# A graph network in one kernel: GpSimd's indirect transfers, at most two under way

## The chip, the cores and the metric

One core of a Trainium2 chip. The metric is the device time of one execution in microseconds. The engines are TensorE (PE, with its weight loads as PEld), VectorE (DVE), ScalarE (ACT), GpSimd (POOL) and SyncE (SP); 16 DMA engines move data between HBM and the on-chip memory (SBUF).

## What is computed

Four layers over 3750 nodes of 256 features and 60000 edges, each added to its input:

```python
x = x + _L0_gnn_ref(_layernorm(x), W, attn_l, attn_r, h_bias, src, dst, edge_type_8)  # attention over edges
x = x + _L0_ffn_ref(_layernorm(x)[None], ...)[0]                                     # shared MLP + 2 of 4 experts
x = x + _L1_gnn_ref(_layernorm(x), edge_attr_20, ..., edge_index)                    # convolution over edges
x = x + _L1_ffn_ref(_layernorm(x)[None], ...)[0]                                     # 2 of 16 experts
```

The two graph layers:

```python
feat_all = jnp.einsum('ni,rhid->rnhd', inputs, conv_weights)       # 8 relations, 4 heads of 64
e = leaky_relu(sum(feat_all[typ, src] * attn_l[typ]) + sum(feat_all[typ, dst] * attn_r[typ]))
alpha = softmax of e over the edges of each dst, per head
h = segment_sum(alpha * feat_all[typ, src], dst) + h_bias

filt = silu(rbf @ Wf1 + bf1) @ Wf2 + bf2                           # per edge
msg = x[col] * filt;  agg = segment_sum(msg, row)                  # then an MLP and a batch norm
```

## The kernel before

**Tiles.** Nodes lie in 30 tiles of 128. Edges are sorted on the chip into bins by the tile of their target node (for the attention) and of their source node (for the convolution). A bin is padded to a multiple of 512 edges, so that a group of `K = 4` tiles of 128 edges belongs to one node tile. A table of sorted edge records has `ET = 588` tiles, 147 groups. `fill` and `fill1` first write both tables with empty records (L541 to L548): all of them carry one and the same row address, 3750 in the first table and 0 in the second. Places that no edge takes stay so, some at the end of each bin and a longer stretch at the end of the table.

**Who moves rows.** All gathers and scatters by computed address are indirect transfers that GpSimd issues, one for 128 rows:
- `Sender` (L276) scatters edge records into a table, a column of 128 edges at a time, in batches of 8 on two semaphores in turn, so that up to 16 are under way. For table 0 it sends 20 columns beside `rank` "by_src", 44 in the first layer norm (beside `fill1`, 28 writes of 252 KB, L1956) and 405 in `project`. For table 1 it sends the last 37 columns in `mixture`.
- `project` (L603) computes the features of all nodes and relations into `feat` in HBM, with 30 stores of 1040 KB from SyncE (L639). It ends when its engines and its sender have ended.
- `attend` (L726) runs through the 147 groups as a software pipeline over steps. GpSimd gathers four tiles of `feat` rows (128 x 260 floats, 130 KB) into one of three buffers `got` (L806), and scatters three columns of table 1 (L812) per group from the fourth group on. The gathers of a group wait until the group three before it has been used up: `f_ready` from DVE (L925, which reads the buffer's first half) and `last_ready` from ACT (L957, the second half). One semaphore for each buffer counts its four gathers. DVE reads the gathered rows first at L895.
- `convolve` (L1331) gathers four tiles of `xtab` rows (128 x 256 floats, 128 KB) per group (L1402), again into three buffers, after both of DVE's multiplications L1507 of the group three before (`msg_ready`). TensorE's largest part is L1454.
- `routed` (L1646) scatters token numbers to `slots` (L1710, 60 transfers, batches of 10), gathers 76 tiles of tokens (L1788, two buffers) and combines the results with 60 gathers (L1891, 12 buffers).

**Order.** Every engine has a program of its own, with waits on semaphores written out by hand. A stage ends in a barrier of all engines. GpSimd runs its transfers in the order written. Its instruction ends when the descriptors have been made, and the data land later; the transfer then adds 16 to its semaphore.

## Time and profile before

| | |
|---|---|
| median of 3 runs | 4172.16 us (4170.39 to 4174.0) |
| profiled execution | 4176.44 us, span 4174.7 us |
| busy | PE 2928.3, PEld 2364.7, DVE 2177.3, ACT 1210.5, POOL 2277.2 us |
| granted TensorE clock, mean | 0.858 of full |
| DMA | 317.71 MB, 76 GB/s |

The stages in the span, roughly: edge keys and ranks to 103 us, first layer norm to 165, projection to 700, attention to 2030, join and first feed-forward layer to 2420, convolution to 3300, update and routing to 3620, experts to 4079, combination and store to the end. The busy time of GpSimd is that of making descriptors. A share of busy time over the whole span says little here, as each stage has a limit of its own. In the rows below, "idle before" an instruction is put down to what released it; "issue" means that the profile shows nothing that it waited for.

### The profile page before, as it was taken

The numbers are of one execution on the slowest core, as the hardware profiler recorded it, in microseconds if no ns is written. First come the engines' busy times: TensorE is split into PE (matmuls) and PEld (weight loads), VectorE is DVE, ScalarE is ACT, GpSimd is POOL, SyncE is SP. The second block draws the span as 40 slices with busy tenths as digits, with TensorE's granted clock in tenths as the row PEclk, the third lists the DMA queues.
The fourth block names the chain that finished last, engine by engine and source line by source line (L and its number), as shares of the span: only waits on it lengthen the run. The fifth ranks groups of instructions, "written<-read, shape, count | busy, mean of one in ns | idle before, by whom it ended". The sixth has DMA issues, their size and how long they took to land. (4 is left out here: it accounts for less than half of the span.)

```text
span 4174.7 us, 73619 instructions
## 1 busy us (share of the span) xinstructions
PE 2928.3 (70%) x20296; PEld 2364.7 (57%) x20297; DVE 2177.3 (52%) x5961; ACT 1210.5 (29%) x3266; POOL 2277.2 (55%) x2336
## 2 busy tenths in 40 slices
PE   5199101777777777776379679999999864299990
PEld 1188101555555555555255358888888633288990
DVE  8411002877777777777743557777777444011112
ACT  1123000444444444444223223333333231022220
POOL 2777775777777777777240056666666200511115
PEclk8599655998998999999679789999999875599995
DMA  3344101222222222225100143333335501155533
GB/s 105 108 135 137 40 2 32 63 65 63 63 64 63 64 64 63 64 64 62 23 19 1 47 136 89 90 89 90 90 90 84 52 0 39 49 175 173 171 104 114
DMA packets 209214, 317.71 MB, mean 76 GB/s; under 512 B 63367, under 2 KB 150063, under 8 KB 208388
## 3 DMA queue, kind: packets, MB, share of 16 engines
q0 software_dynamic: 95008, 179.89, 19.9%
q1 hardware_dynamic: 103204, 127.24, 9.4%
q10 hardware_dynamic: 10944, 9.97, 0.7%
q8 instruction: 17, 0.28, 0.0%
q14 instruction: 41, 0.34, 0.0%
HBM read 248.03 MB, written 68.84 MB: 76 GB/s over the span
## 5 line engine op out<-in xcount | busy, mean ns | idle before, releaser
L1402 POOL DMA_INDIRECT conv_got<-xtab,conv_rowidx x588 | 565.8, 962 | 313.2 <-DVE conv_msg L1507 156.6
L806 POOL DMA_INDIRECT att_got<-feat,att_rowidx x588 | 573.2, 975 | 201.5 <-issue 150.2
L294 POOL DMA_INDIRECT table<-l0a_rec,l0a_addr x469 | 458.2, 977 | 216.7 <-issue 146.1
L1454 PE MATMUL conv_pf<-conv_wf,conv_act 128*128 128x256 f32 x2352 | 534.0, 380 | 0.2 <-DVE conv_filt L1502 0.2
L812 POOL DMA_INDIRECT table<-recs_rec,recs_addr x432 | 423.2, 980 | 131.6 <-issue 130.4
L1454 PEld LDWEIGHTS conv_pf<-conv_wf,conv_act 128*128 128x128 f32 x2352 | 447.6, 190 | 76.9 <-issue 0.8
L982 PE MATMUL att_pmax<-all_identb,att_away 128*128 128x512 bf16 x588 | 261.1, 444 | 203.9 <-DVE att_elo L901 203.2
L863 DVE TENSOR_REDUCE att_tmax<-att_pmax 128x4 f32<-128x512 f32 x588 | 373.8, 680 | 31.1 <-PE att_pmax L986 27.6
L986 PE MATMUL att_pmax<-all_identb,att_ehi 128*128 128x128 bf16 x2352 | 383.6, 242 | 0.0
L986 PE MATMUL att_pmax<-all_identb,att_elo 128*128 128x128 bf16 x2352 | 383.3, 242 | 0.0
L1420 ACT ACTIVATE conv_act<-conv_p,conv_bf 128x512 f32<-128x512 f32 x294 | 186.2, 684 | 552.1 <-PE conv_p L1446 552.1
L1502 DVE TENSOR_TENSOR conv_filt<-conv_pf,conv_bf 128x512 f32<-128x512 f32 x294 | 202.8, 691 | 222.1 <-PE conv_pf L1454 222.1
L986 PEld LDWEIGHTS att_pmax<-all_identb,att_elo 128*128 128x128 bf16 x2352 | 260.5, 111 | 93.0 <-issue 41.6
L1013 PE MATMUL att_psum<-att_f,att_onehot 128*128 128x260 f32 x1176 | 303.7, 403 | 1.9 <-DVE att_f L925 1.9
L1873 DVE TENSOR_TENSOR moe_hid<-moe_gatev,moe_p 128x512 f32<-128x512 f32 x76 | 52.2, 687 | 484.4 <-ACT moe_gatev L1853 484.4
L1825 PE MATMUL moe_p<-moe_xT,moe_w 128*128 128x128 f32 x2432 | 287.5, 277 | 17.4 <-issue 7.1
L957 ACT ACTIVATE att_f<-att_got,att_ex 128x64 f32<-128x64 f32 x1176 | 294.5, 333 | 0.0
L1825 PEld LDWEIGHTS moe_p<-moe_xT,moe_w 128*128 128x128 f32 x2432 | 278.7, 193 | 23.5 <-issue 18.3
L1463 PE MATMUL conv_psum<-conv_msg,conv_onehot 128*128 128x256 f32 x1176 | 279.0, 380 | 5.6 <-DVE conv_msg L1507 5.6
L1788 POOL DMA_INDIRECT moe_got<-xtab,moe_tokens x76 | 72.0, 948 | 368.2 <-PE moe_pT L1814 358.6
L706 PE MATMUL proj_ps<-proj_w,proj_xs 128*128 128x260 f32 x960 | 220.1, 388 | 74.6 <-DVE proj_wr L652 70.0
L986 PEld LDWEIGHTS att_pmax<-all_identb,att_ehi 128*128 128x128 bf16 x2352 | 260.0, 111 | 0.0
(336 smaller groups left out, 5074.0 us busy)
## 6 DMA issues: line engine op xcount, KB each, us to landing
moe_w<-in_L_ffn_w SPq DMA_DIRECT2D x96, 512.0 KB
feat<-proj_out SPq DMA_DIRECT2D x30, 1040.0 KB
results<-moe_y ACTq DMA_DIRECT2D x76, 128.0 KB, 1.7
att_got<-feat,att_rowidx POOLq DMA_INDIRECT x588
conv_got<-xtab,conv_rowidx POOLq DMA_INDIRECT x588, 2.8
xtab<-ln_row SPq DMA_DIRECT2D x60, 128.0 KB, 1.7
table<-l0a_rec,l0a_addr POOLq DMA_INDIRECT x469
table<-recs_rec,recs_addr POOLq DMA_INDIRECT x469, 2.1
```

The costliest lines, as they stand in the source:

```text
L294: self.nc.gpsimd.indirect_dma_start(out=self.table, out_offset=bass.IndirectOffsetOnAxis(ap=self.addrs[:, j:j + 1], axis=0), in_=self.recs ...
L806: nc.gpsimd.indirect_dma_start(out=got[g % 3][:, k, :], out_offset=None, in_=feat, in_offset=bass.IndirectOffsetOnAxis(ap=rowidx[:, g * K ...
L812: nc.gpsimd.indirect_dma_start(out=table1, out_offset=bass.IndirectOffsetOnAxis(ap=addr1[:, i:i + 1], axis=0), in_=rec1[:, i, :], in_offse ...
L863: count(v.tensor_reduce(tmax[:, k, :], pmax[k][:, :, :], AX.X, ALU.max))
L957: nc.scalar.activation(f[s2][:, k, h, 0:HD], got[s2][:, k, h * HD:(h + 1) * HD], ACT.Copy, scale=ex[:, k, h:h + 1]).then_inc(last_ready, 1)
L982: nc.tensor.matmul(pmax[k][:, :, :], away[s1][:, k, :], bcast(c["identb"][:, :], [[0, HEADS], [1, P]]), start=True, stop=False, skip_group ...
L986: ins = nc.tensor.matmul(pmax[k][:, h, :], part[s1][:, k, h:h + 1].broadcast_to([P, P]), c["identb"][:, :], start=False, stop=(part is elo ...
L1013: ins = nc.tensor.matmul(psum[:, 0:HEADS * H1], oh[s2][:, k, :], flat(f[s2][:, k, :, :]), start=(k == 0), stop=(k == K - 1))
L1402: nc.gpsimd.indirect_dma_start(out=got[g % 3][:, k, :], out_offset=None, in_=xtab, in_offset=bass.IndirectOffsetOnAxis(ap=rowidx[:, g * K ...
L1454: ins = nc.tensor.matmul(pf[b][:, k, :], act1[s3][:, h, (2 * b + k) * P:(2 * b + k + 1) * P], wf2[:, h, :], start=(h == 0), stop=(h == 1))
L1463: ins = nc.tensor.matmul(psum[s4][:, 0:D], oh[s4][:, k, :], msg[s4][:, k, :], start=(k == 0), stop=(k == K - 1))
L1825: ins = nc.tensor.matmul(ps[w][:, j * P:(j + 1) * P], wt[w][:, k, j * P:(j + 1) * P], xT[w][:, k, :], start=(k == 0), stop=(k == 1))
```

## The change

A class `Transfers` keeps the list of the indirect transfers that GpSimd has begun in a stage, each with its semaphore and the count at which it has landed. `room()`, called before a transfer, waits for the landing of the one two before it; `begun()` enters it. It is used in `Sender`, `attend`, `convolve` and the `send` stage of `routed`, and not in the `moe` and `comb` stages. So that each of two transfers under way can be waited for by itself, every tile of a gathered group gets its own semaphore (`got_s[slot][k]`), and the scatters alternate between semaphores. DVE waits for the four semaphores of a group one by one; ACT's wait for the gathered rows is gone. The waits for free buffers are split: in `attend` the first two gathers wait for `f_ready` and the last two for `last_ready`; in `convolve` each pair waits for one of the two `msg_ready` of the group three before. In each of these places the wait for the buffer stands first and `room()` after it.

```diff
+class Transfers:
+    LIMIT = 2
+    def __init__(self, pool):
+        self.pool, self.counts, self.order = pool, {}, []
+    def room(self):
+        if len(self.order) >= self.LIMIT:
+            self.pool.wait_ge(*self.order[-self.LIMIT])
+    def begun(self, name, sem):
+        self.counts[name] = self.counts.get(name, 0) + 16
+        self.order.append((sem, self.counts[name]))
 class Sender:
-    BATCH = 8
...
+        under_way = Transfers(pool)
+        for i in range(self.columns):
+            j, u = self.first + i, i % Transfers.LIMIT
+            under_way.room()
+            self.nc.gpsimd.indirect_dma_start(
+                out=self.table, out_offset=..., in_=self.recs[:, j, :], in_offset=None).then_inc(self.sent[u], 16)
+            under_way.begun(u, self.sent[u])
...
 attend, gpsimd:
+            under_way = Transfers(pool)
             for g in range(GROUPS):
-                if g >= SLOTS:
-                    pool.wait_ge(f_ready, g - 2)
-                    pool.wait_ge(last_ready, (g - 2) * LAST)
                 for k in range(K):
+                    if g >= SLOTS and k == 0:
+                        pool.wait_ge(f_ready, g - 2)
+                    if g >= SLOTS and k == ON_DVE:
+                        pool.wait_ge(last_ready, (g - 2) * LAST)
+                    under_way.room()
                     nc.gpsimd.indirect_dma_start(
-                        out=got[g % 3][:, k, :], ...).then_inc(got_s[g % 3], 16)
-                if g >= 2 * SLOTS:
-                    pool.wait_ge(sent[g % 3], 16 * ROUND * (g // 3 - 1))
+                        out=got[g % 3][:, k, :], ...).then_inc(got_s[g % 3][k], 16)
+                    under_way.begun((g % 3, k), got_s[g % 3][k])
                 for i in range(max(g - SLOTS, 0) * ROUND, max(g - SLOTS + 1, 0) * ROUND):
+                    under_way.room()
                     nc.gpsimd.indirect_dma_start(
-                        out=table1, ...).then_inc(sent[g % 3], 16)
+                        out=table1, ...).then_inc(sent[i % 3], 16)
+                    under_way.begun(i % 3, sent[i % 3])
 attend, vector:
-                    dve.wait_ge(got_s[s1], ((i + 1) if u else i) * 16 * K)
+                    for k in range(K):
+                        dve.wait_ge(got_s[s1][k], ((i + 1) if u else i) * 16)
 attend, scalar:
-                    act.wait_ge(got_s[s2], ((i + 1) if u == 2 else i) * 16 * K)
 convolve, gpsimd:
+            under_way = Transfers(pool)
             for g in range(GROUPS):
-                if g >= SLOTS:
-                    pool.wait_ge(msg_ready, (g - 2) * 2)
                 for k in range(K):
+                    if g >= SLOTS and k % 2 == 0:
+                        pool.wait_ge(msg_ready, (g - SLOTS) * 2 + k // 2 + 1)
+                    under_way.room()
...
 convolve, vector:
-                    dve.wait_ge(got_s[s3], i * 16 * K)
+                    for k in range(K):
+                        dve.wait_ge(got_s[s3][k], i * 16)
 routed, send, gpsimd:
+                under_way = Transfers(pool)
                 for i in range(2 * NT):
-                    if batch >= 2 and i % BATCH == 0:
-                        pool.wait_ge(sent[batch % 2], 16 * BATCH * (batch // 2))
+                    under_way.room()
```

## Rows read from the trace of the kernel before

**Rows 1.** Page, part 5: GpSimd's costliest groups (busy, mean ns, idle before).
```profile
L1402 POOL DMA_INDIRECT conv_got<-xtab,conv_rowidx x588 | 565.8, 962 | 313.2 <-DVE conv_msg L1507 156.6
L806 POOL DMA_INDIRECT att_got<-feat,att_rowidx x588 | 573.2, 975 | 201.5 <-issue 150.2
L294 POOL DMA_INDIRECT table<-l0a_rec,l0a_addr x469 | 458.2, 977 | 216.7 <-issue 146.1
L812 POOL DMA_INDIRECT table<-recs_rec,recs_addr x432 | 423.2, 980 | 131.6 <-issue 130.4
```
**Rows 2.** Windows by stage: length, then each engine's busy time; clock; DMA share; GB/s.
```profile
206.00:442.00 236.00, 227.93 (x1074) 196.76 (x1073) 44.18 (x120) 69.39 (x177) 178.10 (x186) 1.00 0.43 136
442.00:688.00 246.00, 0.00 (x0) 0.00 (x0) 0.00 (x0) 0.00 (x0) 184.28 (x192) 0.50 0.03 3
725.00:1873.00 1148.00, 826.52 (x8782) 659.08 (x8780) 883.03 (x3096) 487.17 (x1673) 874.05 (x897) 0.92 0.27 64
2442.00:3180.00 738.00, 738.00 (x3792) 633.18 (x3791) 532.45 (x1139) 258.18 (x506) 487.70 (x508) 1.00 0.35 90
3180.00:3285.00 105.00, 104.66 (x536) 89.40 (x534) 72.24 (x153) 35.45 (x68) 66.60 (x69) 1.00 0.81 79
```
**Rows 3.** Waits: total us, times, longest.
```profile
DVE att_z L895 <- DMA att_got<-feat,att_rowidx: 221.8, 127, 4.1
...
POOL att_got L806 <- ACT att_f L957: 34.5, 94, 6.1
```
**Rows 4.** Timeline of GpSimd and DVE in the attention: start, us, instruction.
```profile
1509.81 0.95 POOL L806 DMA_INDIRECT att_got<-feat,att_rowidx  x1 [0.30 <-issue]
1512.71 0.17 DVE L895 TENSOR_TENSOR att_z<-att_ers,att_got 128x16 f32<-128x16 f32 x1 [1.54 <-DMA att_got<-feat,att_rowidx]
1514.91 0.98 POOL L806 DMA_INDIRECT att_got<-feat,att_rowidx  x1 [0.30 <-issue]
...
1523.82 0.98 POOL L806 DMA_INDIRECT att_got<-feat,att_rowidx  x1 [0.30 <-issue]
```
**Rows 5.** Landing: page part 6; tiles conv_got (2442:3180, 2600:2604, 3225:3284) and comb_got.
```profile
table<-recs_rec,recs_addr POOLq DMA_INDIRECT x469, 2.1
...
DMA to landing us min/median/max: 2.6/2.8/5.3
DMA to landing us min/median/max: 3.9/4.1/4.6
DMA to landing us min/median/max: 10.0/13.4/14.4
DMA to landing us min/median/max: 2.7/2.7/2.8
```
**Rows 6.** Timeline in the convolution: DVE's messages and GpSimd behind them.
```profile
2701.62 1.28 DVE L1507 TENSOR_TENSOR conv_msg<-conv_filt,conv_got 128x512 f32<-128x512 f32 x2
2703.18 0.95 POOL L1402 DMA_INDIRECT conv_got<-xtab,conv_rowidx  x1 [1.08 <-DVE conv_msg L1507]
...
2709.01 0.95 POOL L1402 DMA_INDIRECT conv_got<-xtab,conv_rowidx  x1 [1.08 <-DVE conv_msg L1507]
```
**Rows 7.** Timeline at the attention's fourth group: ACT, then GpSimd.
```profile
723.13 2.00 ACT L957 ACTIVATE att_f<-att_got,att_ex 128x64 f32<-128x64 f32 x8
725.91 0.94 POOL L806 DMA_INDIRECT att_got<-feat,att_rowidx  x1 [6.11 <-ACT att_f L957]
```
**Rows 8.** Windows around one store of `feat`, and GpSimd's scatters beside it.
```profile
229.00:230.00 1.00, 1.00 (x6) 0.85 (x6) 0.00 (x0) 0.39 (x1) 0.70 (x2) 1.00 0.64 198
...
232.00:233.00 1.00, 1.00 (x6) 0.86 (x5) 0.00 (x0) 0.51 (x2) 0.96 (x1) 1.00 0.73 187
228.24 0.96 POOL L294 DMA_INDIRECT table<-l0a_rec,l0a_addr  x1 [0.31 <-issue]
...
230.77 0.96 POOL L294 DMA_INDIRECT table<-l0a_rec,l0a_addr  x1 [0.30 <-issue]
```
**Rows 9.** Windows of the first layer norm.
```profile
103.00:125.00 22.00, 4.12 (x20) 3.86 (x20) 18.67 (x50) 4.31 (x11) 16.49 (x18) 0.51 0.96 329
145.00:158.00 13.00, 0.00 (x0) 0.00 (x0) 0.00 (x0) 0.00 (x0) 9.76 (x11) 0.50 0.03 2
```

More of the change, by code:

```diff
@@ L283, in __init__ @@
         self.first, self.columns = first, columns
-        self.sent = [s.sem(f"sent{u}") for u in range(2)]
+        self.sent = [s.sem(f"sent{u}") for u in range(Transfers.LIMIT)]
     def __call__(self, pool):
-        batches = [range(i, min(i + self.BATCH, self.columns)) for i in range(0, self.columns, self.BATCH)]
-        done = [0, 0]
-        for n, batch in enumerate(batches):
-            u = n % 2
-            wait_positive(pool, self.sent[u], done[u])
-            for i in batch:
-                j = self.first + i
-                self.nc.gpsimd.indirect_dma_start(
-                    out=self.table, out_offset=bass.IndirectOffsetOnAxis(ap=self.addrs[:, j:j + 1], axis=0),
-                    in_=self.recs[:, j, :], in_offset=None).then_inc(self.sent[u], 16)
-            done[u] += 16 * len(batch)
-        for u in range(2):
-            wait_positive(pool, self.sent[u], done[u])
+        under_way = Transfers(pool)
[3 more added lines that the diff above has]
+            self.nc.gpsimd.indirect_dma_start(
+                out=self.table, out_offset=bass.IndirectOffsetOnAxis(ap=self.addrs[:, j:j + 1], axis=0),
+                in_=self.recs[:, j, :], in_offset=None).then_inc(self.sent[u], 16)
+            under_way.begun(u, self.sent[u])
+        for u in range(Transfers.LIMIT):
+            wait_positive(pool, self.sent[u], 16 * len(range(u, self.columns, Transfers.LIMIT)))
 def layer_norm(nc, name, c, x_res, xnT, table=None, add=False, side=None, fill=None):
@@ L766, in attend @@
         loaded, prep, dv = s.sem("loaded"), s.sem("prep"), s.sem("dv")
-        got_s = [s.sem(f"got_s{u}") for u in three]
+        got_s = [[s.sem(f"got_s{u}{k}") for k in range(K)] for u in three]
         oh_ready, turned, ohT_ready, away_ready = (s.sem(n) for n in ("oh_ready", "turned", "ohT_ready", "away_ready"))
@@ L1364, in convolve @@
         filt_ready, msg_ready, summed, agg_done = (s.sem(n) for n in ("filt_ready", "msg_ready", "summed", "agg_done"))
-        got_s = [s.sem(f"got_s{u}") for u in three]
+        got_s = [[s.sem(f"got_s{u}{k}") for k in range(K)] for u in three]
         block = s.block()
@@ L1396, in _ @@
             pool.wait_ge(prep, 2)
+            under_way = Transfers(pool)
             for g in range(GROUPS):
[L1399 to L1400 removed]
                 for k in range(K):
+                    if g >= SLOTS and k % 2 == 0:
+                        pool.wait_ge(msg_ready, (g - SLOTS) * 2 + k // 2 + 1)
+                    under_way.room()
                     nc.gpsimd.indirect_dma_start(
                         out=got[g % 3][:, k, :], out_offset=None, in_=xtab,
[L1404 removed]
+                        in_offset=bass.IndirectOffsetOnAxis(ap=rowidx[:, g * K + k:g * K + k + 1], axis=0)).then_inc(got_s[g % 3][k], 16)
+                    under_way.begun((g % 3, k), got_s[g % 3][k])
         @block.scalar
@@ L1693, in routed @@
         with Stage(nc, "send") as s:
-            BATCH = 10
-            assert 2 * NT % (2 * BATCH) == 0
-            sent, dv = [s.sem(f"sent{u}") for u in range(2)], s.sem("dv")
+            LANES = Transfers.LIMIT
+            assert 2 * NT % LANES == 0
+            sent, dv = [s.sem(f"sent{u}") for u in range(LANES)], s.sem("dv")
             block = s.block()
@@ L1704, in _ @@
             def _(pool):
+                under_way = Transfers(pool)
                 for i in range(2 * NT):
-                    t, k, batch = i // 2, i % 2, i // BATCH
+                    t, k = i // 2, i % 2
                     n = P if t < NT - 1 else TAIL
-                    if batch >= 2 and i % BATCH == 0:
-                        pool.wait_ge(sent[batch % 2], 16 * BATCH * (batch // 2))
+                    under_way.room()
                     nc.gpsimd.indirect_dma_start(
                         out=slots, out_offset=bass.IndirectOffsetOnAxis(ap=addr_i[0:n, k * NT + t:k * NT + t + 1], axis=0),
-                        in_=token[0:n, t:t + 1], in_offset=None).then_inc(sent[batch % 2], 16)
-                for u in range(2):
-                    pool.wait_ge(sent[u], 16 * NT)
+                        in_=token[0:n, t:t + 1], in_offset=None).then_inc(sent[i % LANES], 16)
+                    under_way.begun(i % LANES, sent[i % LANES])
+                for u in range(LANES):
+                    pool.wait_ge(sent[u], 16 * (2 * NT // LANES))
         with Stage(nc, "moe") as s:
```

7 lines of the change are left out of this document (3 added, 4 removed).

## Prediction

> **What bounds the kernel now.** I read the page first, for the GpSimd groups: four lines issue 2,077 of the indirect transfers, each busy for 0.96 to 0.98 us [rows 1]. I then cut the span by stage, to see who is full in each [rows 2]. In the projection (206 to 442) TensorE is full, but the stage goes on to 688 with GpSimd alone. In the attention (725 to 2016) no compute engine is full: DVE 77%, TensorE 72%. In the convolution (2442 to 3285) TensorE is busy all the time. The waits settle the attention: GpSimd's gaps are mostly "issue" (it waits for nothing) [rows 1], while DVE waits 221.8 us for gathers [rows 3]. The timeline shows the beat [rows 4]: a transfer each 1.25 to 1.30 us, say 1.27, seven in a group of 8.91 us (1514.91 to 1523.82). So GpSimd's issue bounds the attention and the tail of the projection. In the convolution GpSimd waits 156.6 us for DVE's messages [rows 1]: four transfers of 1.25 and a gap of 0.78 make 5.84 us (2703.18 to 2709.01 [rows 6]), which is TensorE's time.
>
> **The limit, in general.** A transfer may begin when the one two before it has landed. Without the limit two transfers take 2 x 1.27 = 2.54 us, so it costs nothing as long as landing plus waking GpSimd stay under that. Landing is counted from the instruction's start. A gather takes 2.8 us in the convolution and 2.7 in the last stage, a scatter 2.1 [rows 5]. For the attention's gather the trace gives no landing, but DVE's L895 starts at 1512.71 on the one issued last, at 1509.81 [rows 4]: 2.90 with DVE's own start, so 2.8 again.
>
> Waking has two prices. A transfer with one wait starts 0.28 us after its releaser's end: DVE ends at 2702.90, GpSimd starts at 2703.18 [rows 6]. With two waits, where the one written second comes last (L804, `last_ready`, at the fourth group), ACT ends at 725.13 and GpSimd starts at 725.91: 0.78 us [rows 7]. My reading is that the first wait rides on the transfer, already handed to the engine, and the second stops the hand-over, so that it begins only when the wait is met. That counts here: in the diff the buffer wait is written first and `room()` second, at k = 0 and 2 in both stages.
>
> So the distance from a transfer to the next but one is at least:
> - scatter, one wait: 2.1 + 0.28 = 2.4 us, under 2.54: free.
> - gather, one wait: 2.8 + 0.27 = 3.07 us.
> - gather, limit as second wait: 2.8 + 0.77 = 3.57 us.
> - scatter, limit as second wait: 2.1 + 0.78 = 2.9 us.
>
> **Attention.** One group in order, G for gather, S for scatter: G0 at 0; G1 at 1.27; G2, whose second wait is G0's landing, at 3.57; G3 1.27 later, 4.84; S0 waits for G2, 3.57 + 3.07 = 6.64; S1 7.91; S2 9.18; the next G0 has S1's landing as its second wait, 7.91 + 2.9 = 10.8. That is 10.8 in place of 8.91, +1.88 us in each of 144 groups: +271 us. All of it is on the path, since nothing but GpSimd bounds the stage. The first three groups issue no scatters and their 12 gathers take some 3 us longer, but GpSimd idled 6.11 us behind them [rows 7], which covers it. The half-group waits take away only waits that cost little now (34.5 us in all [rows 3], nearly all as normal 0.30 gaps): nothing gained.
>
> Some gathers land late. The last 100 us of the convolution land at 13.4 us, and four gathers at 2599 to 2603 at 4.1 [rows 5]. These are groups of padding, whose rows all carry the same address (the memsets of the empty tables), at the end of the table and at the end of a bin. I take about 28 such groups in each stage: 16 at the end (3183 to 3283) and the rest at the ends of bins (an estimate: landings like the two shown recur at the ends of bins). Alone such a gather takes some 3.75 us, so each of the two pairs in a group costs 0.95 more: 28 x 1.9 = +53 us. Attention: +324 us; bounds +197 (below) and +347.
>
> **Convolution.** A group is two pairs, each opened by a gather with `room()` as second wait: 2 x 3.57 = 7.14 us, against 5.84 of TensorE. GpSimd becomes the bound: +1.28 x 144 = +184 us. Padding groups: 28 x 1.8 = +50, but the 16 at the end already run at some 6.6 us now, 0.76 over the beat, so -12. And the last gather landed up to 14.4 us after its issue where it will take 4: -10. Sum +212 us.
>
> **Projection and first layer norm (`Sender`).** Each transfer has one wait and a landing of 2.1 us: free, except beside large transfers. Line 639 stores 1040 KB 30 times; in one store the DMA engines are 0.64 busy and more for four microseconds, 229 to 233 [rows 8]. The scatter issued at 228.24 and the one after it land only when it is over, at about 233.4 (estimate: the end of that stretch and a little). Now GpSimd goes on issuing at 230.77; with the limit it starts at 233.4 + 0.28, 2.9 us later. Over the phases at which a store can begin I take 2.5, bounds 2.3 and 3.3: 30 x 2.5 = +75 us (69 to 99), all on the path, as GpSimd ends this stage alone [rows 2]. In the layer norm 18 scatters run beside the fill of table 1, DMA share 0.96 [rows 9]; a landing of 3.4 us (estimate, between 2.1 and 5.2) makes each 0.5 longer: +8 us, and there too GpSimd is the last one working, 145 to 158.
>
> **Edits at nothing.** `Sender` beside `rank` and in the mixture: 20 and 37 transfers behind DVE and TensorE work. The 60 scatters to `slots`: single wait, 2.1 us landing, DMA engines idle. Their first and last waits are the old ones. DVE's four semaphores in place of one: three more waits a group, at some 0.05 to 0.1 us each, on an engine that waits for the gathers anyway; if that cover went, 147 x 0.2 = 30 us a stage. ACT's wait taken away: `ex_ready` implied it. The combine stage has no limit and stays as it is.
>
> **Sum.** 324 + 212 + 75 + 8 = 619 us on the profiled execution's 4176.4 gives 4795.6; the median of the runs is 4.3 us below that execution, so 4791.
>
> **A rule of the skill.** The trace's gather of 128 KB takes 2.8 us, in two stages [rows 5]. The Trainium skill, DMA: Bandwidth & Descriptors, section Anatomy of one DMA, gives about 2.0 us plus the bytes by 436 GB/s for a transfer from GpSimd, 2.3 us for this one. The trace does not agree; by the page's figure the pairs would be 2.57 and 3.07 us, and the whole about 4500 (the attention +128 and 53 for padding, the convolution +43 and 28, the senders 83). The same page (section Latency and other measured facts) says that a lighter load on HBM makes the fixed part smaller. Both make the third rival.
>
> **Rivals.**
> 1. The limit's wait costs 0.28 everywhere (as if it were the one that rides on the transfer). For it: only one place in the trace shows the 0.78. Against: the delay is clean there. The attention's group is then 9.93 us (+1.0 x 144 = 147, with padding 197), the convolution's 6.12 (+40, with padding and end 68): 4172 + 197 + 68 + 83 = 4520 us. Chance 0.13.
> 2. TensorE's clock. In the attention it is 0.92 of full with TensorE 72% busy; in the convolution 1.00 at 100% [rows 2]. With GpSimd as bound, TensorE is at 59% and 82%. If the clock went as in the attention's present rows, work in the half-speed stretches doubles, still below the new groups. Should a fifth of the groups run at 1.2 GHz throughout, TensorE would need 12.8 us a group in the attention (826.52 of 1148 us is 6.4 of 8.91, doubled) and 11.7 in the convolution: 29 x (2.0 + 4.6) = +191, about 4980 us. Chance 0.06.
> 3. Landing depends on how many transfers are under way. With two, a gather might land in 2.3 us; then the pairs are 2.57 (one wait) and 3.07 (two), the attention's group 9.8 and the convolution's 6.14, and the time about 4500. Chance 0.04. Not slower at all: from a landing of 2.54 - 0.77 = 1.77 us on, the limit never decides for a gather, nor under 2.26 where it is the one wait; the time stays 4172. Against both: the landings are 2.6 at the least over the whole regular stretch, gaps in GpSimd's issue included, and the gathers of the last stage, up to twelve at once, land in 2.7 [rows 5]; depth does not show. Chance of the second 0.02.
> 4. The change does not limit (waits met in advance). The counts in `Transfers` ask for the full 16 per transfer, so no. Chance 0.01, 4172.
>
> **How the numbers follow.** Forecast as summed, 0.74. Its own range: low, 0.6 us in place of 0.77 for the second wait and landings of 2.7 (some -130); high, the upper bounds of padding and stores (+23, +24) and 30 for DVE: 4660 to 4870. For 8 in 10 I reach a little towards rivals 1 and 2: 4620 to 4890. A measurement of this kernel tells 0.2% apart. Faster than that 0.01, within it 0.03, slower 0.96.
>
> **What would show it.** Right: attention groups 10.8 us apart and convolution groups 7.1; GpSimd's gaps in them put down to its own transfers' landing, not "issue"; gaps at k = 2 longer than at k = 1; scatters in 442 to 688 still 1.27 apart; TensorE no longer full in the convolution. Wrong: groups at 9.9 and 6.1 (rival 1), TensorE full with a clock near 0.5 (2), gathers landing much under 2.7 (3).

## Result: slower by 15.9%, and the profile after

| | before | after |
|---|---|---|
| median | 4171.27 us (4 runs, 4166.4 to 4174.0) | 4833.34 us (4 runs, 4829.8 to 4837.9) |
| ratio | | 1.159, interval 1.157 to 1.161 |
| profiled execution, span | 4176.44, 4174.7 us | 4831.86, 4830.1 us |
| granted clock of TensorE, mean | 0.858 | 0.828 |

The instructions and the bytes are the same (317.74 MB against 317.71), and the busy times of DVE, ACT and GpSimd moved by less than 30 us. TensorE's grew from 2928.3 to 3136.8 us, under a granted clock of 0.828 in place of 0.858; it is not what bounds the long stages now, as the windows below show. What made the kernel longer are GpSimd's gaps. First the page of the changed kernel, part 5, GpSimd's groups (busy, mean ns, idle before, releaser), and part 6, the time from issue to landing. The lines answer to [rows 1] and [rows 5].

```profile
PE 3136.8 (65%) x20296; PEld 2445.8 (51%) x20297; DVE 2174.6 (45%) x5961; ACT 1217.9 (25%) x3266; POOL 2305.3 (48%) x2336
...
L1421 POOL DMA_INDIRECT conv_got<-xtab,conv_rowidx x588 | 572.2, 973 | 527.9 <-DMA conv_got<-xtab,conv_rowidx 430.8
L822 POOL DMA_INDIRECT att_got<-feat,att_rowidx x588 | 564.7, 960 | 407.1 <-DMA att_got<-feat,att_rowidx 219.3
...
L307 POOL DMA_INDIRECT table<-l0a_rec,l0a_addr x469 | 456.4, 973 | 314.9 <-issue 130.3
L828 POOL DMA_INDIRECT table<-recs_rec,recs_addr x432 | 455.7, 1055 | 258.1 <-DMA att_got<-feat,att_rowidx 193.5
...
att_got<-feat,att_rowidx POOLq DMA_INDIRECT x588, 2.8
conv_got<-xtab,conv_rowidx POOLq DMA_INDIRECT x588, 2.8
...
table<-recs_rec,recs_addr POOLq DMA_INDIRECT x469, 2.1
```

GpSimd's idle time ahead of these four groups is 1508.0 us (527.9 + 407.1 + 314.9 + 258.1), where it was 863.0 [rows 1]: 645.0 more, and the profiled execution is 655.4 us longer. The releaser has changed from "issue" to GpSimd's own gathers. The landings are what they were.

The timeline of GpSimd over one group of the attention, in the changed kernel. It is the beat that [rows 4] showed for before.

```profile
1502.83 0.97 POOL L822 DMA_INDIRECT att_got<-feat,att_rowidx  x1 [0.48 <-issue]
1504.11 0.96 POOL L822 DMA_INDIRECT att_got<-feat,att_rowidx  x1 [0.30 <-issue]
1506.39 0.95 POOL L822 DMA_INDIRECT att_got<-feat,att_rowidx  x1 [1.33 <-DMA att_got<-feat,att_rowidx]
1507.65 0.95 POOL L822 DMA_INDIRECT att_got<-feat,att_rowidx  x1 [0.30 <-issue]
1509.42 1.00 POOL L828 DMA_INDIRECT table<-recs_rec,recs_addr  x1 [0.82 <-DMA att_got<-feat,att_rowidx]
1510.72 0.97 POOL L828 DMA_INDIRECT table<-recs_rec,recs_addr  x1 [0.30 <-DMA att_got<-feat,att_rowidx]
1512.00 1.20 POOL L828 DMA_INDIRECT table<-recs_rec,recs_addr  x1 [0.30 <-issue]
1513.65 0.97 POOL L822 DMA_INDIRECT att_got<-feat,att_rowidx  x1 [0.46 <-issue]
```

Read the starts as distances from the first: 0, 1.28, 3.56, 4.82, 6.59, 7.89, 9.17, and the next group at 10.82. The forecast was 0, 1.27, 3.57, 4.84, 6.64, 7.91, 9.18, 10.8. The 1.33 us of idle time at the third gather is the limit behind a second wait; the 0.82 at the first scatter is the limit as the only wait.

What the other engines make of it, in windows of the changed kernel by stage (length, then busy time of PE, PEld, DVE, ACT and POOL, clock, DMA share, GB/s; they answer to [rows 2]):

```profile
206.00:442.00 236.00, 227.43 (x1060) 196.04 (x1061) 46.63 (x118) 68.99 (x176) 118.96 (x124) 0.98 0.41 131
442.00:790.00 348.00, 4.12 (x22) 3.51 (x20) 1.47 (x4) 0.77 (x2) 253.84 (x265) 0.51 0.04 6
830.00:2240.00 1410.00, 905.36 (x8596) 714.88 (x8596) 872.53 (x3036) 484.33 (x1642) 879.61 (x880) 0.84 0.21 51
...
2880.00:3730.00 850.00, 760.75 (x3584) 586.09 (x3583) 489.71 (x1070) 245.28 (x480) 457.37 (x471) 0.98 0.27 73
```

In the projection's first window GpSimd issues 124 transfers where it issued 186 [rows 2]; the missing 62 are sent when nobody else works any more. The stage boundaries, read from GpSimd's first and last instruction of each line, put the loss in its places:

| stretch | before, us | after, us | difference | forecast |
|---|---|---|---|---|
| first layer norm to the projection's sender | 103.3 to 165.2 | 103.7 to 173.1 | +7.5 | +8 |
| projection, to the first gather of the attention | to 704.2 | to 800.7 | +88.6 | +75 |
| attention and what follows, to the convolution | to 2422.0 | to 2863.9 | +345.4 | +324 |
| convolution and update, to `slots` | to 3537.4 | to 4192.1 | +212.8 | +212 |
| rest | to the end | to the end | +0.7 | 0 |

### The profile page after: what moved, and what is told of

Its sections match the earlier page's. It is cut to its first block and busy times, and to the rows that moved or that the text cites. A ratio compares the mean times of both kernels' runs of the same rounds, so it can differ in the third digit from the quotient of the medians.

```text
span 4830.1 us, 74107 instructions
## 1 busy us (share of the span) xinstructions
PE 3136.8 (65%) x20296; PEld 2445.8 (51%) x20297; DVE 2174.6 (45%) x5961; ACT 1217.9 (25%) x3266; POOL 2305.3 (48%) x2336
## 2 busy tenths in 40 slices
DMA packets 209217, 317.74 MB, mean 66 GB/s; under 512 B 63367, under 2 KB 150063, under 8 KB 208388
## 5 line engine op out<-in xcount | busy, mean ns | idle before, releaser
L1421 POOL DMA_INDIRECT conv_got<-xtab,conv_rowidx x588 | 572.2, 973 | 527.9 <-DMA conv_got<-xtab,conv_rowidx 430.8
L822 POOL DMA_INDIRECT att_got<-feat,att_rowidx x588 | 564.7, 960 | 407.1 <-DMA att_got<-feat,att_rowidx 219.3
L999 PE MATMUL att_pmax<-all_identb,att_away 128*128 128x512 bf16 x588 | 315.6, 537 | 466.8 <-DVE att_elo L919 466.7
L307 POOL DMA_INDIRECT table<-l0a_rec,l0a_addr x469 | 456.4, 973 | 314.9 <-issue 130.3
L828 POOL DMA_INDIRECT table<-recs_rec,recs_addr x432 | 455.7, 1055 | 258.1 <-DMA att_got<-feat,att_rowidx 193.5
L1003 PE MATMUL att_pmax<-all_identb,att_ehi 128*128 128x128 bf16 x2352 | 463.5, 274 | 0.0
L1003 PE MATMUL att_pmax<-all_identb,att_elo 128*128 128x128 bf16 x2352 | 461.5, 274 | 0.0
L1528 DVE TENSOR_TENSOR conv_msg<-conv_filt,conv_got 128x512 f32<-128x512 f32 x294 | 191.7, 693 | 449.9 <-DMA conv_got<-xtab,conv_rowidx 449.9
L1003 PEld LDWEIGHTS att_pmax<-all_identb,att_elo 128*128 128x128 bf16 x2352 | 303.4, 129 | 127.8 <-issue 102.8
L1483 PEld LDWEIGHTS conv_psum<-conv_msg,conv_onehot 128*128 128x128 f32 x1176 | 225.8, 201 | 183.5 <-issue 154.9
L999 PEld LDWEIGHTS att_pmax<-all_identb,att_away 128*128 128x128 bf16 x588 | 73.3, 125 | 479.7 <-DVE att_elo L919 479.7
L1003 PEld LDWEIGHTS att_pmax<-all_identb,att_ehi 128*128 128x128 bf16 x2352 | 302.2, 128 | 0.0
L1847 PE MATMUL moe_p<-moe_xT,moe_w 128*128 128x128 f32 x2432 | 288.6, 277 | 16.8 <-issue 10.8
L1010 PE MATMUL att_pT<-all_identb,att_away 128*128 128x128 bf16 x588 | 63.0, 235 | 359.7 <-ACT att_away L968 359.7
```

The source lines that it names most:

```text
L307: self.nc.gpsimd.indirect_dma_start(out=self.table, out_offset=bass.IndirectOffsetOnAxis(ap=self.addrs[:, j:j + 1], axis=0), in_=self.recs ...
L822: nc.gpsimd.indirect_dma_start(out=got[g % 3][:, k, :], out_offset=None, in_=feat, in_offset=bass.IndirectOffsetOnAxis(ap=rowidx[:, g * K ...
L828: nc.gpsimd.indirect_dma_start(out=table1, out_offset=bass.IndirectOffsetOnAxis(ap=addr1[:, i:i + 1], axis=0), in_=rec1[:, i, :], in_offse ...
L999: nc.tensor.matmul(pmax[k][:, :, :], away[s1][:, k, :], bcast(c["identb"][:, :], [[0, HEADS], [1, P]]), start=True, stop=False, skip_group ...
L1003: ins = nc.tensor.matmul(pmax[k][:, h, :], part[s1][:, k, h:h + 1].broadcast_to([P, P]), c["identb"][:, :], start=False, stop=(part is elo ...
L1421: nc.gpsimd.indirect_dma_start(out=got[g % 3][:, k, :], out_offset=None, in_=xtab, in_offset=bass.IndirectOffsetOnAxis(ap=rowidx[:, g * K ...
```

## Experiments

Kernels of one batch ran on one chip, beside the kernel before; every ratio is to the kernel before of the same batch. This matters: swap, limit3, sender_only and no_limit ran on a chip on which the kernel before takes 4172 us. The other kernels ran on two chips on which the same kernel before takes 5252 to 5277 us. Times of different batches on the first kind of chip are compared directly, as the kernel before takes 4171 to 4172 us in both; otherwise only where the text says so. Line numbers differ by a few between the kernels.

### Is the second wait the dearer one? (swap)

```diff
+                    under_way.room()
                     if g >= SLOTS and k == 0:
                         pool.wait_ge(f_ready, g - 2)
                     if g >= SLOTS and k == ON_DVE:
                         pool.wait_ge(last_ready, (g - 2) * LAST)
-                    under_way.room()
```
The same in `convolve`. The waits are the same ones, in the other order.

> The changed kernel with room() written ahead of the wait for the buffer, in the attention (k = 0 and 2) and in the convolution (k = 0 and 2). The limit of two stays. Theory (the wait written second stops the hand-over and costs 0.78 us in place of 0.28): the attention's group falls from 10.8 to about 9.95 us, the convolution's from 7.05 to about 6.15, and the time from 4833 to about 4560 us. Rival (the place of a wait does not matter, all is landing time): groups and time stay, 4833 us.

Measured: 4620.22 us, ratio 1.1075 (1.1057 to 1.1094), so 213 us less than the changed kernel for two lines exchanged. The convolution's groups are 6.07 us apart (7.05 in the changed kernel); the attention's 10.36 (10.89), where 9.95 was expected. The timeline of swap tells what the attention kept, first GpSimd, then DVE:

```profile
1502.51 1.08 POOL L822 DMA_INDIRECT att_got<-feat,att_rowidx  x1 [0.30 <-issue]
1503.89 0.96 POOL L822 DMA_INDIRECT att_got<-feat,att_rowidx  x1 [0.31 <-ACT att_f L974]
1505.63 0.94 POOL L822 DMA_INDIRECT att_got<-feat,att_rowidx  x1 [0.78 <-DMA att_got<-feat,att_rowidx]
...
1511.30 1.20 POOL L828 DMA_INDIRECT table<-recs_rec,recs_addr  x1 [0.30 <-issue]
1512.81 1.09 POOL L822 DMA_INDIRECT att_got<-feat,att_rowidx  x1 [0.30 <-issue]
```
```profile
1510.98 0.69 DVE L929 TENSOR_TENSOR att_onehot<-all_ramp,att_recs 128x512 f32<-128x512 f32 x1
1511.59 0.85 DVE L865 SCALAR_TENSOR_TENSOR l_acc<-l_acc,att_keep,att_psum 128x65 f32 x4
1512.36 0.68 DVE L943 TENSOR_TENSOR att_f<-att_got,att_ex 128x512 f32<-128x512 f32 x1
```

The idle time at the third gather is 0.78 us where it was 1.33. Part of that difference is the longer first gather beside it (1.08 us). From the landing of the gather two before to the start of the third, the two traces have 0.77 us with the limit as second wait and 0.26 with the limit written first, in the median of the attention's groups whose landing is recorded, and 0.76 and 0.26 in the convolution. So the price of the second wait is 0.51 us a place, where [rows 7] against [rows 6] gave 0.50. But the third scatter now takes 1.20 us and the first gather 1.08, where the others take 0.94 to 1.0. In the changed kernel the scatter was as long, yet a wait of the next gather covered it; here it is on the path. DVE works without a break beside it.

### Is it DVE that makes the scatter long? (swap_small_oh)

```diff
-  v.tensor_tensor(oh[u][:, :, :], bcast(c["ramp"][:, 0:P], [[0, K], [1, P]]), ...
+  kk = K if isinstance(t, int) else 1
+  v.tensor_tensor(oh[u][:, 0:kk, :], bcast(c["ramp"][:, 0:P], [[0, kk], [1, P]]), ...
```

> The kernel of the run swap; in the attention's loop DVE writes one tile of the one-hot matrix per group in place of four (128 elements in place of 512), so the other three keep the contents of an earlier group and the result is not the reference's. Theory (in swap the third scatter of each group takes 1.2 us in place of 0.96, because DVE's one-hot, accumulation and L943 then run without a gap; GpSimd's own descriptor work is what stands on the path there): the third scatter falls to under 1.1 us and the attention's group from 10.36 to 10.1 to 10.2 us; 4590 us. Rival (the length of the third scatter has nothing to do with DVE): 1.2 us and 10.36 us stay.

Measured: the third scatter takes 0.971 us in the mean, against 1.215 in swap. The groups are 12.1 us apart here, so DVE no longer works beside that scatter in every group, and the two means alone would not separate the length of DVE's run from its place. The trace does: 52 of the attention's transfers lie beside the four accumulations (L865 above; at least 0.8 us of them), and these take 0.976 us in the mean, where 140 such in swap take 1.224. With a quarter of the one-hot ahead of it, DVE's run no longer stretches a transfer. The kernel before has such transfers too, 44 of them, up to 1.48 us long, 1.107 in the mean.

The time, 4881.3 us in one run on a chip of the second kind, says nothing on the 30 us that I expected from it beside swap: there TensorE has idle time in the attention that the profile puts down to nothing (129.7 us at att_per, 51.0 at att_pT), as the last part of this section shows. It does say that swap's order of the waits did not bring this kernel under the changed kernel on such a chip (4874.93 us, below).

### How deep must the queue be? (limit3, limit1)

```diff
-    LIMIT = 2
+    LIMIT = 3
```

> The changed kernel with LIMIT = 3. Theory (only landing plus waking against the issue of the transfers between counts): three issues take 3.8 us, more than the 3.57 us of a gather with the dearer wait, so the regular groups are back at 8.9 and 5.84 us; left are the padding groups (some 30 us) and the scatters beside the stores of feat (some 50 us): about 4250 us. Rival (the waits themselves slow GpSimd down, whatever the depth): attention groups clearly above 9 us, time over 4400 us.

Measured: 4261.63 us, ratio 1.0219 (1.0202 to 1.0236). Attention groups are 8.90 us apart and convolution groups 5.84, both as before. What is left of the 90 us is 45.7 in the projection, whose stores still hold up the third transfer, and the padding: the last 16 groups take 10.5 us in the attention and 6.68 in the convolution. One transfer more gives back 86% of the loss (572 of 662 us).

```diff
-    LIMIT = 2
+    LIMIT = 1
```

> The changed kernel with LIMIT = 1: every transfer waits for the landing of the one before. Theory (distance = landing plus waking, 3.07 us for a gather, 3.57 where the limit is the second wait behind a gather, 2.4 for a scatter, 2.9 as second wait): attention group 2.9 + 3.07 + 3.57 + 3.07 + 3.07 + 2.4 + 2.4 = 20.5 us, convolution group 3.57 + 3.07 + 3.57 + 3.07 = 13.3 us, a scatter of the projection each 2.4 us; the time 4172 + 1670 + 1075 + 200 (padding) + 507 (senders) + 68 (slots) = about 7690 us. Rival (landing shortens when only one transfer is under way): landings clearly under 2.6 us, groups of 18 us or less.

Measured: 7819.87 us in one run. Attention groups 20.89 us apart (20.5 expected), convolution groups 13.04 (13.3). The convolution's gathers as a tile, in the changed kernel over the regular stretch and in limit1 over all:

```profile
L1421 POOL DMA_INDIRECT conv_got<-xtab,conv_rowidx x471: 940/946/1467, 2879.4 to 3729.8; - x157
...
DMA to landing us min/median/max: 2.7/2.8/4.4
```
```profile
L1421 POOL DMA_INDIRECT conv_got<-xtab,conv_rowidx x588: 944/944/1267, 4850.4 to 6868.4; - x196
...
DMA to landing us min/median/max: 2.6/2.8/4.0
```

A gather lands after 2.8 us whether it is alone, one of two, or one of three. More than three were never under way in the regular stretches of the kernel before either, at a landing of 2.8 us and a beat of 1.27, whatever its buffers allowed. The third rival falls.

### Projection and senders alone (sender_only)

```diff
 attend, convolve, gpsimd:
-                    under_way.room()
-                    under_way.begun((g % 3, k), got_s[g % 3][k])
+                if g >= 2 * SLOTS:
+                    pool.wait_ge(sent[g % 3], 16 * ROUND * (g // 3 - 1))
```
The limit stays in `Sender` and in `send`.

> The changed kernel without the limit in the attention and the convolution (their semaphores and half-group waits stay); the limit of two stays in Sender and in the scatters to slots. Theory: only the projection and the first layer norm are longer, by the 96 us by which the attention starts later in the changed kernel: about 4268 us. My forecast had 83 us here: 4255. Rival (the delay of the attention's start comes from something else in the change): 4172 us.

Measured: 4260.86 us, 1.0219 (1.0202 to 1.0236), 89 us over before, 7 under the expectation. The attention starts at 802.6 us, 98.4 later than before, so some ten come back later. That limit3 gives the same ratio is a coincidence of other parts: 45.7 us by the attention's start there, 98.4 here.

### The rest of the diff alone (no_limit)

```diff
-                    under_way.room()
-                    under_way.begun(...)
 Sender, send: as in the kernel before
```
What stays: a semaphore for each gather, the waits for half the buffers, DVE's four waits and ACT's missing one.

> The change without its limit anywhere: one semaphore for each gathered tile, DVE's four waits, ACT's wait gone, half-group waits; senders as before. Theory (these edits cost nothing): 4172 us, within 0.2%. Rival a (DVE's three more waits in each group count, some 0.2 us in the convolution and the attention): up to 4230 us. Rival b (the half-group waits help): under 4160 us.

Measured: 4164.1 us, 0.9993 (0.9972 to 1.0015). These edits cost nothing, as costed, and what they bring is within the interval: the median is 8 us under the kernel before, and in the trace the stretch from the end of the attention's last scatter to the convolution's first gather takes 396.3 us in place of 405.0. The whole loss is the limit's.

### Padding with one and the same address (spread_after, spread_before)

```diff
+  nc.gpsimd.iota(spread_i[:, :], pattern=[[0, 1]], base=0, channel_multiplier=29)
-  nc.gpsimd.memset(empty0[:, :, 0:1], float(NODES))
+  nc.gpsimd.tensor_copy(empty0[:, :, 0:1], bcast(spread[:, :], [[0, ET], [0, 1]]))
+  nc.gpsimd.tensor_copy(empty1[:, :, NG:NG + 1], bcast(spread[:, :], ...))
```
The empty records of a tile now point to 128 different rows; their edges still count for nothing.

> The changed kernel, but the empty records of both tables carry 128 different row addresses (29 times the partition) in place of one and the same. Theory (the late gathers are those of padding, whose 128 rows all lie at one address): all gathers land in 2.6 to 2.9 us, groups at the end of the tables are as long as the others (10.85 and 7.05 us), and the time falls by about 28 x 2.3 + 28 x 1.7 = 112 us, to about 4720. Rival (the end of the stages is slower for another reason, such as the queue or the number of rows): 4833 us and 13.1 us groups at the end.

Measured: 4771.32 us on the second kind of chip. The last 16 groups are 10.99 us apart in the attention and 7.12 in the convolution, as the regular ones; in the changed kernel they are 13.1 and 8.78. The tile of the convolution's gathers near the end of the table, the changed kernel first (gathers, their first and last start; how long the later ones waited for them; landing), then spread_after:

```profile
L1421 POOL DMA_INDIRECT conv_got<-xtab,conv_rowidx x48: 940/945/1215, 3779.8 to 3878.8; - x48
...
  POOL conv_got L1421: 50.9, 36
...
DMA to landing us min/median/max: 2.7/3.6/4.2
```
```profile
L1428 POOL DMA_INDIRECT conv_got<-xtab,conv_rowidx x60: 940/946/1462, 3779.8 to 3884.0; - x60
...
  POOL conv_got L1428: 35.7, 28
```

The changed kernel sends 48 gathers in 99 us, spread_after 60 in 104. So the one shared address is the cause. Against the unaltered changed kernel on another chip of this kind (4874.93 us, below) it is 104 us, where the two padding terms of my sum, 53 and 50, make 103.

> The kernel before with the same 128 addresses in the empty records. Theory: in the attention nothing changes, since GpSimd issues at its own beat whatever the landing; in the convolution the last gathers land in 2.8 us in place of 14, and TensorE stays the bound: 10 to 15 us less, 4160 us. If late landing cost the kernel before more than its last gather: under 4140 us.

Measured: 5329.07 us, against 5252.47 for the kernel before on that chip, ratio 1.015 (1.008 to 1.023). I had expected 4160 for a kernel before of 4172. That is 77 us more than the kernel before on its chip, and not the 10 to 15 less of the theory. Nothing in the edit explains a number of 5300; the kernel before itself took 1080 us more on this chip. That opened the question of the next part.

### The same kernels on another chip (round2, best, after_again, robust)

round2 is the kernel before with two scatters a group in the attention in place of three; best is no_limit with that and with the spread addresses; robust is swap with LIMIT = 3, two scatters a group and the spread addresses; after_again is the changed kernel, unaltered.

```diff
-ROUND = 3
+ROUND = 2
```

> The kernel before with ROUND = 2: two scatters of table 1 per group of the attention in place of three, 181 in place of 37 behind it in the mixture. Theory (the attention is bound by the number of transfers that GpSimd issues): the group is 6 x 1.27 = 7.63 us in place of 8.91, -182 us; the mixture's sender needs 230 us and ends some 38 us after the mixture ends now: about 4030 us. Rival (DVE or TensorE is close behind GpSimd in the attention): groups over 8.2 us, time over 4100 us.

> The kernel of the run no_limit with ROUND = 2 and with 128 different addresses in the empty records. Theory: the gain of round2 and 10 to 15 us from the convolution's end: about 4015 us.

> The changed kernel once more, unaltered, timed beside the kernel before, because in two jobs, with five other kernels, the kernel before took 5252 and 5260 us and no longer 4172, with stretches in which TensorE stands still without a wait. Theory (the chips differ: on some, many transfers under way hold up the other engines, most of all while the projection's scatters run): where before takes 4172 us the changed kernel takes 4833; where before takes about 5250 us it takes 4830 to 4900, and is the faster one. Rival (such a chip slows every kernel alike): there it would take 5250 x 1.159 = 6085 us.

> The changed kernel with LIMIT = 3, room() ahead of the buffer waits, 128 different addresses in the empty records, and ROUND = 2 (two scatters per attention group, 181 in the mixture). Theory: landing plus waking (3.07 us) is under three issues (3.8), so the attention's group is 6 x 1.27 = 7.63 us and the convolution's 5.84; the senders beside the stores cost 46 us. Where before takes 4172 us: 4172 + 46 - 182 + 38 - 12 = 4062 us. Where before takes 5250 us: below the changed kernel, some 4400, if three transfers under way are few enough to leave TensorE alone; if they are not, stalls of TensorE without a wait and over 4800.

| kernel | transfers allowed under way | us | ratio to before on its chip |
|---|---|---|---|
| before | up to 16 | 5252 to 5277 | 1 |
| spread_before | up to 16 | 5329.07 | 1.015 (1.008 to 1.023) |
| round2 | up to 16 | 5117.35 | 0.973 (0.967 to 0.979) |
| best | up to 16 | 5061.49 | 0.961 (0.955 to 0.967) |
| robust | 3 | 5008.64 | 0.948 (0.943 to 0.952) |
| after_again | 2 | 4874.93 | 0.924 (0.921 to 0.928) |
| spread_after | 2 | 4771.32 | 0.909 (0.904 to 0.914) |

The times that I had expected of round2 (4030 us) and best (4015) were for a chip of the first kind, and these runs don't test them. Their groups are not 7.63 us apart: 11.4 in round2, 11.2 in best, 11.6 in robust.

On such a chip the change makes the kernel faster by 7.6%, the same text that makes it slower by 15.9% on the first. The changed kernel itself moved by 0.9% between the two kinds (4833.34 to 4874.93), the kernel before by 26%. After_again's groups are 10.90 and 7.05 us apart, as on the first chip.

Where the kernels without a limit lose it is in the waits of TensorE put down to "issue", that is to nothing that the profile shows (total us, times, longest). First spread_before, then round2, then best:

```profile
PE proj_ps L713 <- issue: 392.9, 8, 75.7
PE att_pmax L993 <- issue: 265.8, 309, 1.9
```
```profile
PE proj_ps L706 <- issue: 407.0, 8, 75.7
...
PE att_pmax L986 <- issue: 213.2, 319, 1.3
```
```profile
PE proj_ps L713 <- issue: 406.3, 8, 75.6
...
PE att_pmax L994 <- issue: 81.0, 125, 1.2
```

And with the limit, robust (3) first, then after_again (2):

```profile
PE att_pmax L1010 <- issue: 52.2, 110, 1.1
...
PE proj_ps L726 <- issue: 3.9, 23, 0.4
```
```profile
PE att_pmax L999 <- issue: 89.1, 67, 4.7
...
PE proj_ps L719 <- issue: 2.8, 18, 0.2
```

In the projection's matmuls, 393 to 407 us of it become 3.9 and 2.8. With one under way (limit1, a chip of the second kind too) no row of the attention or the projection has it. The timeline of TensorE in the projection shows what it means, spread_before first, after_again below:

```profile
287.55 8.85 PE L713 MATMUL proj_ps<-proj_w,proj_xs 128*128 128x260 f32 x28 [48.59 <-issue]
...
388.37 7.94 PE L713 MATMUL proj_ps<-proj_w,proj_xs 128*128 128x260 f32 x28 [74.95 <-issue]
```
```profile
238.32 7.28 PE L719 MATMUL proj_ps<-proj_w,proj_xs 128*128 128x260 f32 x32 [0.16 <-issue]
```

The gaps of 49 to 75 us look like idle time without a cause, but ACT's and DVE's copies of the products tell what TensorE stood for. ACT copies the first five products of a node tile, DVE the last three; here they are in spread_before between two of TensorE's runs:

```profile
320.69 0.39 ACT L687 ACTIVATE proj_out<-proj_ps 128x260 f32<-128x260 f32 x1 [10.11 <-remote]
...
343.09 0.39 ACT L687 ACTIVATE proj_out<-proj_ps 128x260 f32<-128x260 f32 x1 [10.81 <-remote]
354.29 0.39 ACT L687 ACTIVATE proj_out<-proj_ps 128x260 f32<-128x260 f32 x1 [10.81 <-remote]
...
376.69 0.43 DVE L667 COPY proj_out<-proj_ps 128x260 f32<-128x260 f32 x1 [10.77 <-remote]
387.89 0.43 DVE L667 COPY proj_out<-proj_ps 128x260 f32<-128x260 f32 x1 [10.77 <-remote]
```

A product is four matmuls, so by TensorE's records seven of the eight products were done at 296.40 (287.55 + 8.85). Each copy waits for its product's count on one semaphore ("remote": the profile finds no instruction that ended just before the count rose). The counts come 11.20 us apart, the one for the seventh product 80 us after its matmuls; in after_again the copies start 0.88 us apart. Each copy starts 0.03 us after its count, and TensorE's next run starts at 388.37, 0.05 us after the copy of the last product, which gives it its buffer back. So TensorE does wait, for DVE, and DVE and ACT wait for TensorE's own signals, which reach them late or belong to products that were late; as the ends of matmuls are modelled, the trace doesn't tell these two apart. When the last scatter has been issued, at 727, the stage is back at its old beat within some 35 us.

And the windows of spread_before over the stage (columns as above):

```profile
182.00:727.00 545.00, 72.84 (x252) 58.94 (x252) 27.17 (x32) 15.29 (x40) 408.72 (x404) 0.55 0.09 21
727.00:952.00 225.00, 177.91 (x828) 153.29 (x828) 42.11 (x99) 54.83 (x140) 1.08 (x1) 0.90 0.34 119
```

As long as GpSimd sends its 404 transfers, TensorE is busy 72.84 us of 545. It does three quarters of its instructions after them, so that work which lay side by side now lies end to end, and the attention begins at 952.5 us where it began at 704.2. With two under way TensorE is at its full 232.13 us of 254:

```profile
206.00:460.00 254.00, 232.13 (x1080) 200.00 (x1080) 48.77 (x123) 69.46 (x178) 130.39 (x134) 0.96 0.39 127
```

What is shown: on these chips TensorE's signals come up to 80 us after the matmuls, and TensorE stands for up to 76 us for that, while GpSimd issues its scatters in one unbroken row; it does not in the projection of the kernels with a limit. Why the signals are late stays open. Against a late supply of instructions speaks that each copy, and TensorE's next run, starts within 0.05 us of what it waits for.

Nor do the runs show that it is the number under way. The steps by which a landing scatter counts up its semaphore come 1.94 us after its start in the median in spread_before and 2.00 in the kernel before, and the beat is 1.27 us in both, so away from the stores of `feat` two are under way, with the limit and without it; "up to 16" in the table is what the kernel allows. Nor is it enough that the limit puts a wait ahead of each transfer, even where it is met in advance. Robust's `Sender` has these waits in the mixture too. There its 181 scatters go out 1.28 us apart without a break, and TensorE has the same steps of 11.2 us again: it restarts at 2801.2, 2812.5, 2823.7, 2834.9 and 2846.1. One of these rows:

```profile
2823.67 1.54 PE L1233 MATMUL mixf_bank<-mixf_h,mixf_e2w 128*64 128x384 f32 x2 [9.66 <-issue]
```

What the disturbed stretches share is the unbroken beat; in the projection of the kernels with a limit the stores break it. That is a reading: no run breaks the beat and changes nothing else.

The table isn't a scale of depth either. Robust, whose projection is undisturbed, took 1727 us from the attention's first gather to its last where after_again took 1664, with groups of 11.6 us for an expected 7.63. From there to the convolution's first gather it took 621 us against 441: its mixture sends 181 scatters and not 37, and TensorE has idle time put down to nothing there (117.6 us in the mixture's matmuls, up to 43.7 at a time). My reading for robust (4400 if three were few enough) fell. Nor do the runs tell whether it is the chip or something that runs beside it, nor is there a trace of the unaltered kernel before on such a chip; spread_before stands for it.

## Why the prediction was right, and where it was off

The time was forecast as 4791, measured 4833 (range 4620 to 4890). On the profiled execution the sum was 619 and the difference 655.4.

- **The distances in a group.** Right to 0.05 us at every place of the one timed group. The step that carried it was the price of a second wait, read from one place [rows 7]. Swap shows it apart: 0.77 against 0.26 us from landing to start, 213 us of the total. Rival 1 (0.28 everywhere, 4520 us) falls. Why a second wait costs more (the prediction's hand-over) no run shows; only its price is measured. That the order of two waits is worth 5% of the kernel, on the chip of the forecast, is the most useful number of this case.
- **Attention, +324.** About +356 from GpSimd's first gather to its last scatter, of which 285 are the groups' (10.89 less 8.91, 144 times; I had 271). The padding, where I had 53, is told apart by spread_after: its attention takes 1604.7 us from first to last gather, after_again's 1664.4 on a chip of the same kind, 59.7 more (the changed kernel's on the first chip 1661.9, 57.2 more). So the padding was mis-sized by some 5 us, the regular group by 14, and some 11 to 14 us of irregular groups stood in no term. The last 16 groups took 13.1 us, where 10.8 + 1.9 makes 12.7: such gathers land after 3.8 and 4.1 us in turn and not 3.75. Of the 356, 11 us came back between the attention's last scatter and the convolution; 9 of them come back in no_limit too, so they are the semaphore edits' and not the limit's.
- **Convolution, +212.** Measured +212.8. That it is equal is in part luck: the groups are 7.05 us apart where I had 7.14, which is 10 us less in 144, and the deduction of 12 us for the padding at the table's end was too large, since those groups already ran at 6.07 us and not 6.6. They take 8.78 now. GpSimd is the bound there now: TensorE is busy 760.75 of 850 us, 90% where the prediction had 82%.
- **Projection, +75.** Measured +88.6, inside the bounds 69 to 99; a store costs 2.95 us and not 2.5. The changed kernel's waits give the same: `Sender`'s transfers sat 114.0 us behind their own landings, 49 times; less the normal 0.30 each, 99.3, against the 96.1 of both stages.

```profile
POOL table L307 <- DMA table<-l0a_rec,l0a_addr: 114.0, 49, 4.6
```

- **Edits at nothing.** No_limit: 0.9993. Right, DVE's four waits included.
- **What I missed in the attention.** The third scatter takes 1.19 us (0.96 before), since DVE, which before drifted against GpSimd's beat, now starts each group by the same landings and works beside that scatter nearly every time: 113 of the 144 are over 1.15 us long, before none. In the changed kernel it lies under a wait, 0.46 to 0.48 us of idle time behind it; in swap it is on the path, and there my expectation was 60 us too low.
- **TensorE's clock.** Rival 2 asked for groups that TensorE bounds at the lower of its two levels. The clock did fall in the attention, to 0.84 from 0.92 [rows 2], TensorE being busy 64% of that window (the prediction had 59%), but with 905 of 1410 us busy it was not the bound, and in the convolution it kept 0.98.
- **The rule of the skill.** The Trainium skill, DMA: Bandwidth & Descriptors, section Anatomy of one DMA, gives an estimate of 2.3 us for such a gather; the runs show 2.8 at depths of one, two and more, so the measurement decides. Of the smaller fixed part under a lighter load (section Latency and other measured facts) no run here shows anything. The prediction's argument against the third rival, gathers "up to twelve at once" that land in 2.7 us, was weaker than it reads: at 2.7 us and a beat of 1.27 they were three at once. Limit1 is what settles it.
- **What no rival of mine held.** That the sign depends on the chip. On the chip of the forecast the limit costs 15.9%; where TensorE's signals come late without it, it gains 7.6%. No row of the kernel before [rows 1 to 9] shows a trace of it: TensorE is full in its projection.

No kernel here beats both on both kinds of chip. On the first, no_limit equals before. On the second, the changed kernel with spread addresses is the fastest (0.909). Swap with the limit of two and the spread addresses was not tried there. Its 213 us on the first chip do not carry over unseen: swap_small_oh, which is swap with less work for DVE, took 4881.3 us on such a chip, as long as the changed kernel's 4874.93.

## What to carry to other kernels

A limit on the transfers under way costs nothing as long as landing plus waking (2.8 + 0.28 us for these gathers, 2.8 + 0.77 behind another wait) is shorter than the depth times the issue beat (1.27 us): false at two, true at three, which gave back 86% of the loss. Where one of GpSimd's transfers has two waits, write first the one that is met last: as the second it costs 0.51 us more each time that it decides. And a change in how GpSimd's transfers wait is to be timed on more than one chip before its sign is believed. Idle time that the profile puts down to nothing can still be a wait: read what the other engines did just before it ended.

## Seen of the hardware, and not expected

- On two of the chips TensorE's counts on a semaphore rose 11.20 us apart, up to 80 us after its matmuls by the records, while GpSimd issued scatters 1.27 us apart without a break. TensorE's idle time put down to nothing was 393 to 407 us in the projection, and 81 to 266 at att_pmax in the attention, the kernel before taking 5252 to 5277 us in place of 4172; with the limit of two it was 2.8 and 89 us. The cause is open.
- Gathers of 128 rows with one address land after 3.6 and 4.0 us in turn in the convolution with two under way, those of the regular stretch after 2.8; with 128 different padding addresses the last 16 groups are 7.12 us apart in place of 8.78.
- Making the descriptors of a scatter takes GpSimd 0.96 us, and 1.19 to 1.22 beside an unbroken run of DVE's (one-hot, then four accumulations); 0.98 beside the accumulations when three quarters of the one-hot are left out.
